# A longer ring of buffers between the activation and the split in a mixture-of-experts layer, with a later lag and the first two units put ahead of the router's logits

## What is computed

```python
logits = xf @ wr + br
topk_vals, topk_idx = jax.lax.top_k(logits, K)          # K = 2 of E = 4 experts
gates = jax.nn.softmax(topk_vals, axis=-1)
h = jax.nn.gelu(jnp.einsum('nd,edh->enh', xf, w1) + b1[:, None, :], approximate=False)
y = jnp.einsum('enh,ehd->end', h, w2) + b2[:, None, :]
c = jnp.einsum('eh,ehd->ed', jax.nn.gelu(b1, approximate=False), w2) + b2
out = jnp.einsum('nk,nkd->nd', gates, y_sel - c_sel + c_sum[None, None, :])
```

## Time and profile before

| | us |
|---|---|
| three runs: median (lowest to highest) | 1951.97 (1951.04 to 1957.06) |
| the profiled execution, its time | 1955.56 |
| its span, first to last instruction | 1953.8 |
| busy in that span: PE / DVE / ACT | 1816.8 / 1344.6 / 952.7 |
| expert layer, from its first instruction to the end | 1751.98 to 1953.8 |
| first expert's 16 units on PE, start of the first and last | 1758.62, 1788.52 |
| granted TensorE clock, mean | 0.980 |

### The profile page before, as it was taken

The page is one execution under the profiler, slowest core; times in us unless marked ns, Lnnn a source line. Parts: engine busy times, 40 slices in busy tenths (PEclk is TensorE's granted clock), DMA queues, the critical chain, the costliest instruction groups (busy, mean ns, idle before and its releaser), DMA issues. The chain is left out here.

```text
span 1953.8 us, 31948 instructions
## 1 busy us (share of the span) xinstructions
PE 1816.8 (93%) x10231; PEld 1579.8 (81%) x10231; DVE 1344.6 (69%) x3147; ACT 952.7 (49%) x1661; POOL 602.7 (31%) x647
## 2 busy tenths in 40 slices
PE   5889999999999999999999999999999668768998
PEld 4678888888888888888888888888888567746886
DVE  7576777777777767777777778676776237756666
ACT  4545555554555455555545554555544223324344
POOL 3424334161515243251515153442510014430000
PEclk9899999999999999999999999999999999969999
DMA  8822313131322313131312233131305665202231
GB/s 279 277 62 76 112 39 109 46 101 54 95 78 90 92 65 112 45 101 46 101 58 91 78 95 94 58 112 46 101 22 188 254 249 210 87 1 76 87 107 45
DMA packets 125421, 197.24 MB, mean 101 GB/s; under 512 B 71568, under 2 KB 95024, under 8 KB 119216
## 3 DMA queue, kind: packets, MB, share of 16 engines
q1 hardware_dynamic: 125360, 196.45, 30.3%
HBM read 123.01 MB, written 73.42 MB: 101 GB/s over the span
## 5 line engine op out<-in xcount | busy, mean ns | idle before, releaser
L246 PE MATMUL o_bank<-probT,val 128*128 128x512 f32 x2496 | 685.1, 410 | 7.2 <-DVE probT L884 5.0
L246 PE MATMUL s_bank<-late,qkT 128*128 128x416 f32 x3072 | 628.6, 354 | 11.7 <-DVE qkT L889 9.8
L246 PEld LDWEIGHTS s_bank<-late,qkT 128*128 128x128 f32 x3072 | 572.1, 189 | 42.7 <-issue 11.5
L246 PEld LDWEIGHTS o_bank<-probT,val 128*128 128x128 f32 x2496 | 438.7, 189 | 90.1 <-DVE probT L884 11.6
L848 ACT ACTIVATE prob<-prob,negmax 128x1665 f32<-128x1665 f32 x128 | 216.2, 1689 | 379.5 <-DVE negmax L913 379.5
L884 DVE TENSOR_TENSOR probT<-t_bank,probT 128x512 fp32r<-128x512 f32 x416 | 283.1, 687 | 145.0 <-ACT probT L826 140.2
L826 ACT ACTIVATE probT<-t_bank 128x512 fp32r<-128x512 f32 x416 | 242.4, 590 | 223.1 <-PE t_bank L965 222.9
L908 DVE CUSTOM_DVE_ANT_0 prob<-s_bank,bias 128x416 f32<-128x416 f32 x512 | 296.0, 585 | 70.1 <-PE s_bank L246 68.7
L965 PE MATMUL t_bank<-ident,prob 128*128 128x128 f32 x1664 | 250.4, 273 | 11.3 <-DVE probT L884 7.3
L965 PEld LDWEIGHTS t_bank<-ident,prob 128*128 128x128 f32 x1664 | 205.5, 141 | 52.4 <-DVE probT L884 14.5
L802 POOL TENSOR_TENSOR late_y<-w_raw,late_y 128x1280 fp32r<-128x1280 f32 x16 | 48.2, 3012 | 399.1 <-ACT late_y L820 399.1
(11 more groups left out here) (203 smaller groups left out, 1938.3 us busy)
## 6 DMA issues: line engine op xcount, KB each, us to landing
o_scratch<-outT SPq DMA_DIRECT2D x32, 1024.0 KB, 4.8
stage<-in_ctx SPq DMA_DIRECT2D x48, 512.0 KB, 3.9
w_scratch<-late_y SPq DMA_DIRECT2D x16, 1280.0 KB, 6.4
ffn_w<-o_scratch SPq DMA_DIRECT2D x10, 2048.0 KB, 8.1
qk<-qk_scratch SPq DMA_DIRECT2D x16, 1024.0 KB, 6.8
ffn_w<-w_scratch SPq DMA_DIRECT2D x16, 1024.0 KB, 6.3
late_y<-o_scratch SPq DMA_DIRECT2D x6, 2048.0 KB, 7.3
w_raw<-in_wall SPq DMA_DIRECT2D x16, 640.0 KB, 7.0
```

The source lines that it names most:

```text
L246: mm = pe.matmul(out, weights(a), moving(b), start=first and n == 0, stop=last and n == 2)
```

## The change

The ring has 12 slots: the 7 old ones and 5 in a new tile of 10 KB in each partition. `hid` becomes a list of slots. The first expert's lag is 9 in place of 6; the others keep 3. The copy `gate_rows` moves in ACT's list from step 6 to step 8. On PE the eight transposes to logits move from before hidden(0) to behind hidden(1).

```diff
-HRING = 7
+HRING = 12
...
-    hid = W["stage"][:, :, :].rearrange("p c d -> p (c d)").rearrange("p (r n) -> p r n", r=HRING)
+    own = sb("hid", [P, HRING - 7, 512], F32)
+    kept = W["stage"][:, :, :].rearrange("p c d -> p (c d)").rearrange("p (r n) -> p r n", r=7)
+    hid = [t[:, r, :] for t, n in ((kept, 7), (own, HRING - 7)) for r in range(n)]
...
-            lag = HRING - 1 if e.off == 0 else 3
+            lag = HRING - 3 if e.off == 0 else 3
...
-                if e.off == 0 and m == 6:
+                if e.off == 0 and m == 8:
                     act.wait_ge(gateT_full, 1)
                     act.activation(gate_rows[:, :], gate_bank[0:E4 * RT, 0:P], ACT.Copy).then_inc(gateT_out, 1)
...
-        for t in range(RT):
-            pe.wait_ge(rT_out, 1 + t // 4)
-            mm = pe.transpose(logit_bank[:, t * E4:(t + 1) * E4], rT[:, t * P:(t + 1) * P], ident[0:E4, 0:E4])
-        mm.then_inc(r_full, 1)
+        def logits():
+            for t in range(RT):
+                pe.wait_ge(rT_out, 1 + t // 4)
+                mm = pe.transpose(logit_bank[:, t * E4:(t + 1) * E4], rT[:, t * P:(t + 1) * P], ident[0:E4, 0:E4])
+            mm.then_inc(r_full, 1)
...
             for m in range(2 * HT):
                 hidden(e, m)
+                if e.off == 0 and m == 1:
+                    logits()
```

More of the change, by code:

```diff
@@ L1576, in gelu @@
                 wait(act, h_done, e, 16, m + 1 - HRING)
-                act.activation(hid[:, z, :], hbank[m % 2][:, :], ACT.Gelu, bias=b1[:, e.off, t:t + 1]).then_inc(h_gelu, 1)
+                act.activation(hid[z], hbank[m % 2][:, :], ACT.Gelu, bias=b1[:, e.off, t:t + 1]).then_inc(h_gelu, 1)
             def high(m):
@@ L1581, in high @@
                 wait(act, h_gated, e, 16, m + 1)
-                act.activation(hT[t][:, 0, HALF[half]], hid[:, m % HRING, :], ACT.Copy).then_inc(h_high, 1)
+                act.activation(hT[t][:, 0, HALF[half]], hid[m % HRING], ACT.Copy).then_inc(h_high, 1)
             for m in range(2 * HT + lag):
@@ L1648, in gated @@
                 wait(dve, h_gelu, e, 16, m + 1)
-                dve.scalar_tensor_tensor(out=hid[:, m % HRING, :], in0=hid[:, m % HRING, :], scalar=gb[:, e.off, t:t + 1], in1=g,
+                dve.scalar_tensor_tensor(out=hid[m % HRING], in0=hid[m % HRING], scalar=gb[:, e.off, t:t + 1], in1=g,
                                          op0=ALU.subtract, op1=ALU.mult).then_inc(h_gated, 1)
@@ L1654, in low @@
                 wait(dve, h_high, e, 16, m + 1)
-                dve.tensor_tensor(hT[t][:, 1, HALF[half]], hid[:, m % HRING, :], hT[t][:, 0, HALF[half]].bitcast(F32),
+                dve.tensor_tensor(hT[t][:, 1, HALF[half]], hid[m % HRING], hT[t][:, 0, HALF[half]].bitcast(F32),
                                   ALU.subtract).then_inc(h_done, 1)
```

## The result

| | before | after |
|---|---|---|
| median of five runs | 1952.64 | 1945.62 |
| lowest to highest | 1951.04 to 1957.06 | 1945.01 to 1946.63 |
| profiled execution / its span | 1955.56 / 1953.8 | 1945.64 / 1943.8 |
| mean granted clock of that execution | 0.980 | 0.984 |

The ratio of the runs is 0.995, 95% interval 0.9935 to 0.9965; that of the two medians, which lie 7.0 us apart, is 0.9964. The time forecast, 1946.0, is met to 0.4 us, but its 6.0 us are a ratio of 0.9969, and the interval ends short of that, at 0.9965: the gain measured is larger. The spans of the two profiled executions even differ by 10.0 us. So the first question is what the other 4 us are.

What follows compares the result with a forecast made beforehand. The first expert's units were taken as bound by a 2.02 us round trip over ACT and DVE; 5.6 (ring, lag) plus 0.4 (logits) gave 6.0 us, so 1951.97 - 6.0 = 1946.0, range 1943.6 to 1950.0.

Steps and rivals of the forecast that it cites:

- The bound: First expert's units up to hidden(15): paced by a 2.02 us round trip over ACT and DVE, not either engine's work.
- part 1: Ring of 12 and lag 9: hidden(8) to hidden(15) at PE's 1.36 us a unit, 9.52 for 15.11, gain 5.6 us.
- Part 2: Logits' transposes moved behind hidden(1): gelu(3) and the units behind it start earlier, gain 0.4 us.
- the better bound: Layer's front: at best the first weight load hides and hidden(0) starts 0.14 us earlier, gain 0.55 us.
- the sum: Ring and lag 5.6 plus moved logits 0.4, 6.0 us in all: hidden(15) at 1782.5 in place of 1788.52.
- rival 2: Layer's front: clock rises 1.1 us later or logits come late for exp; gain 5.5 us, 1946.5; chance 0.18.
- the same difference on the median: Profiled execution was 3.6 us above the median of three runs; the median forecast is 1951.97 - 6.0 = 1946.0.
- 1 (the round trip moves): First expert's gelu(12) to gelu(15) wait for low at the old pace; gain 3.3 us, 1948.7; chance 0.16.
- 3 (the clock falls in the idle stretch): PE's idle ahead of hidden(5) drops the clock; each unit costs 1.36 us more, at worst 9 us slower, 1961; chance 0.03.
- 4: Change does nothing, as project waits for something other than hidden(15); chance 0.03.

Runs made afterwards that it cites:

- 12 and 11: Kernel after with 12 slots kept and the first expert's lag 11 in place of 9: median 1950.47, ratio 0.9992 against the kernel before.
- 8 and 6: Kernel after with 8 slots and lag 6, copy of the gate rows in step 6: median 1946.15, ratio 0.9970 against the kernel before.
- 7 and 5: Kernel after with 7 slots and lag 5, no new tile, gate-row copy in step 6: median 1946.98, ratio 0.9982 against the kernel before.
- the repeat: Kernel after, unchanged, run again on a second chip: median 1948.02 (1944.36 to 1950.38), ratio 0.9960 against the kernel before.
- the pooled runs: All 11 runs of the kernel after against those of the kernel before, chips mixed: means 1946.74 and 1953.09.

## Why the prediction was right and wrong

- **The bound and part 1.** Right: 5.6 us forecast, 5.60 in the two traces, 5.63 alone. The pace of 1.36, hidden(8) as the point from which it counts, project without a wait and cacc without effect (it ends at 1800.41, project at 1802.51) all stand as forecast. The rule that came out of it also gave 12 and 11, 8 and 6, and 7 and 5 within 0.2 us. Not seen was that lag and slots are two ways to the same end, and that one slot more was enough.
- **Part 2.** Right in mechanism, 0.1 short: 0.4 forecast, 0.48 and 0.50 measured. The logits came 3.33 us behind the second copy (1757.10 against 1753.77), the maxima in time for the exp, which again waited for nothing but its table load. hidden(0) began 0.20 us ahead of the second copy (1753.57) where I had put it 0.10 ahead (1757.54 against 1757.64), part of the way to the better bound named there.
- **TensorE's clock: the term left out of the sum.** The rise near 1757.3 was priced only as a loss in rival 2, 0.5 us if it came later. It came earlier against the router's matmuls, and the router was never in the sum, since the change leaves it alone. It gave 0.65 us between the two profiles, 0.26 in the repeat (4.88 against 5.14), and another 1.55 in the kernel with extra matmuls. This isn't the change's doing: the kernel before with the unused tile has a router of 4.50 us.
- **Where it went wrong: the step from the sum to the median, "I put the same difference on the median".** I knew of an execution 3.6 us above the median and of three runs 6 us apart, and treated this as noise about an even middle, with 2 us of scatter downwards. (The 1943.6 given as the range's end is 2.4 below 1946.0, not 2.) It is a spread in how long the blocks ahead of the layer take, seen as 1746.55 to 1753.21 in the starts of the layer over the profiles of kernels with the same instructions ahead of it (1748.57 to 1753.21 on one chip), and five runs can all draw from one end: those of the kernel after did, all at a clock of 0.984 or 0.985. A difference of 6.0 then measured as 0.5%, which is 9.8 us, 3.8 more than the sum and 1.4 more than the range had room for (1951.97 to 1943.6 is 8.4), and 0.44 of the chance was on less than 0.3%. That this excess is luck of the draw is supported by the pooled runs, 6.35 us apart with a standard error of 0.64, in which the 6.0 us stand. The chances should have gone by the sum's distance from zero in units of that spread and not by 0.15 us beyond a bound, and the range's lower end by the same.
- **Rivals.** 1 (the round trip moves) is what a lag of 11 does; at 9 it doesn't occur. 2 (the front gives less) didn't occur in the two profiles of the kernel after: the clock stood at 1.00 from 1753 and from 1758 on, ahead of hidden(0) in both. 3 (the clock falls in the idle stretch): PE idled 1.58 us there and hidden(8) to hidden(15) ran at 1.36 each. Its price for a unit was set too high: at a clock of 0.50 the router's weight loads stand 0.43 us apart, so by this estimate a unit of six would have taken 2.6 us, 1.2 more and not 1.36. 4 fell with the first trace. The rule of the Trainium skill, page "TensorE: Matmul & The Clock Gate", Part 1, that the matmuls run at the low clock differ in number from run to run of one kernel, is what the two profiles of the kernel after show: 4.49 and 4.88 us for the same twelve.

## What to carry to other kernels

Where a unit goes to and fro between two engines with lists in fixed order, a round trip of T passes slots minus lag units, so the pace is T / (slots - lag), or the slowest engine's if that is more; here 2.03 / 1 bound and 2.03 / 2 didn't, which one slot, or a shorter lag, would have bought. (The value T / 2 itself was never seen, as PE's 1.36 is longer.) Before a change worth 0.3% is judged by its runs, look at how far one kernel's executions lie apart ahead of the changed place, and compare the stretch itself between two events of its own.

## What was not expected

- The start of the layer moves by 6.7 us (1746.55 to 1753.21) from execution to execution, with the same instructions ahead of it; times go with the mean granted clock, about 5 us from 0.984 and above to 0.978 and below. What sets in an execution when the clock rises stays open, and wasn't tried.
- A table load stands with the instruction that needs it, behind that one's wait (idle 0.73 us); put an instruction of the new table that waits for nothing ahead of it, and it runs early.
- Work without a result can pay: 13 matmuls in idle gaps gave the router 2.94 us in place of 4.49, and the steps just ahead of the layer 15.04 us in place of 15.97.
